# When batches are made ready, who adds the weight blocks, and when TensorE loads its step registers, in a one-core decoder layer

## The reference

```python
x = x + attn(layernorm(x), ...)                  # linear attention, 16 heads
x = x + experts(layernorm(x), itok, ctx, ctx, ctx)   # one of 4 experts per token
x = x + ffn(layernorm(x), W_up, W_gate, W_down)
# experts: e = token id // (25000 // 4)
g = silu(h @ ctx[e].T); u = h @ ctx[e].T; y = (g * u) @ ctx[e].T
# ffn: each weight is clip(round(W / s), -1, 1) * s with s = mean(|W|)
hidden = silu(x @ wu.T) * (x @ wg.T)             # 512 -> 2048
return hidden @ wd.T
```

## Time and profile before

| | |
|---|---|
| time, median of 3 runs | 760.04 us (760.04 to 761.48) |
| profiled execution, its own time / span | 760.04 / 758.1 us |
| PE, PEld, DVE, ACT, POOL busy | 695.5, 457.6, 503.4, 295.2, 250.6 us |
| idle of PE before the region products of line 1482 | 28.5 us in 3 waits |
| experts' stage, first product to first up product | 264.3 to 404.6 us |
| feed-forward stage | 404.6 to 758.1 us |

### The profile page before, as it was taken

One profiled execution on the slowest core, in us unless ns is written; L12 is line 12 of the kernel. 1 busy time (PEld: TensorE's weight loads), 2 busy tenths in 40 slices (PEclk: granted clock), 3 DMA queues, 4 the chain that ended last, 5 costly groups with the idle time before them and its releaser, 6 DMA issues.

```text
span 758.1 us, 12681 instructions
## 1 busy us (share of the span) xinstructions
PE 695.5 (92%) x4745; PEld 457.6 (60%) x4776; DVE 503.4 (66%) x814; ACT 295.2 (39%) x450; POOL 250.6 (33%) x242
## 2 busy tenths in 40 slices
PE   7999999999998799999889999499977999499995
PEld 5565456556564656665447777377755777377772
DVE  5566766766757565567756978388773978457664
ACT  4365554554545244443322433234332343123330
POOL 4204523333334600003640343435431543414222
PEclk9999999999999999999999999899997999899998
DMA  8924035036046587601220030202111120201001
GB/s 246 338 81 142 1 128 206 0 125 208 1 155 234 166 326 253 243 29 42 50 50 1 1 51 1 49 1 81 25 26 25 52 54 1 50 1 56 1 1 55
DMA packets 57910, 67.37 MB, mean 89 GB/s; under 512 B 35072, under 2 KB 35072, under 8 KB 56832
## 3 DMA queue, kind: packets, MB, share of 16 engines
q1 hardware_dynamic: 54016, 54.03, 23.5%
q0 software_dynamic: 3840, 12.59, 4.4%
HBM read 46.69 MB, written 12.59 MB: 78 GB/s over the span
## 4 chain that ended last, share of the span: by engine, by line
PE 74%; DVE 9%; issue 7%; ACT 4%; DMA 2%; SPq 1%; POOL 1%; another core or an unknown queue 0%; POOLq 0%; DVEq 0%; ACTq 0%
PE bank L1211 26%; PE bank L1482 25%; PE bank L1491 13%; PE bank L1204 4%; PE bank L1404 2%; DVE region L829 2%; PE bank L1368 2%; PE bank L1382 2%; DMA w_att<-stage 2%; DVE late L825 1%; DMA stage<-in_L_attn_Wv_dram 1%; ACT stage L639 1%; ACT stage L519 1%; DVE region L833 1%; ACT tmp L527 1%
## 5 line engine op out<-in xcount | busy, mean ns | idle before, releaser
L1482 PE MATMUL bank<-w_att,region 128*128 128x256 f16 x1024 | 130.9, 277 | 28.5 <-issue 28.5
L1482 PEld LDWEIGHTS bank<-w_att,region 128*128 128x128 bf16 x1024 | 101.6, 99 | 48.7 <-issue 29.9
L1491 PE MATMUL bank<-region,w_moe 128*128 128x512 bf16 x481 | 115.5, 383 | 3.9 <-DVE w_moe L1122 2.1
L1132 DVE TENSOR_TENSOR n<-bank,n 128x512 f32<-128x512 f32 x112 | 71.7, 685 | 55.8 <-PE bank L1482 54.2
L1211 PE MATMUL bank<-late,w_att 128*128 128x512 f16 x384 | 86.8, 382 | 2.0 <-DVE region L872 1.9
L445 POOL TENSOR_TENSOR w_moe<-tmp,w_moe 128x512 f16<-128x512 f32 x30 | 36.0, 1200 | 154.3 <-ACT w_moe L669 154.3
L1491 PEld LDWEIGHTS bank<-region,w_moe 128*128 128x128 f16 x512 | 50.5, 99 | 51.2 <-DVE w_moe L1122 2.6
L326 POOL TENSOR_SCALAR ve<-mv 128x1 f32<-128x1 f32 (+2 forms) x29 | 10.9, 377 | 198.4 <-DVE mv L709 198.3
L662 ACT ACTIVATE n<-n,qs 128x512 f32<-128x512 f32 x64 | 44.5, 718 | 71.8 <-DVE n L1132 71.3
L1482 PE MATMUL bank<-w_att,late 128*128 128x256 f16 x512 | 68.6, 279 | 0.0
L1211 PEld LDWEIGHTS bank<-late,w_att 128*128 128x128 f16 x384 | 37.4, 98 | 45.0 <-DVE region L872 2.7
(11 more groups left out here) (161 smaller groups left out, 1143.1 us busy)
## 6 DMA issues: line engine op xcount, KB each, us to landing
stage<-in_L_ffn_W_up_dram SPq DMA_DIRECT2D x8, 1024.0 KB
stage<-in_L_ffn_W_gate_dram SPq DMA_DIRECT2D x8, 1024.0 KB, 5.4
rows<-sorted_residual SPq DMA_DIRECT2D x4, 1026.0 KB, 8.6
stage<-in_ctx_dram SPq DMA_DIRECT2D x4, 1024.0 KB, 6.6
stage<-in_L_ffn_W_down_dram SPq DMA_DIRECT2D x4, 1024.0 KB
nrm<-in_L_ffn_W_down_dram SPq DMA_DIRECT2D x4, 1024.0 KB, 8.0
n<-sorted_tokens SPq DMA_DIRECT2D x16, 256.0 KB, 5.8
rows<-in_x_dram SPq DMA_DIRECT2D x1, 3072.0 KB, 18.6
```

Source lines behind the costliest of these rows:

```text
L1132: dve.tensor_tensor(out, wk_ps[(14 * n + m) % 4][:, :], other, ALU.add).then_inc(s["up_add"], 1)
L1482: mm = pe.matmul(wk_ps[bank][:, q * H:(q + 1) * H], w[:, c + q, k * P:(k + 1) * P], x3S_part[slot][:, h, m, k], start=(h == 0 and k == 0), ...
L1491: mm = pe.matmul(ffy_ps[t][:, :], hid[:, u, h, q, (t % 2) * P:(t % 2 + 1) * P], tern[2][:, c + q], start=(begins and q == 0 and h == 0), s ...
```

## The change

Four things are edited.

1. Batch preparation moves one group ahead: a half is normalised, summed and sent in t = 0 or t = 2 instead of t = 1 or 3, and its stats and rsqrt are one group before that (for half 2 in step 15; for halves 4 and 6 in t = 3 of the batch before).
2. Gate's four weight sums move from GpSimd to VectorE, each beside up's. Of the eight, S1 are in steps 10 and 11, both S3 in 13, both S2 in 16, both S4 in 17, always behind `h_lo`.
3. In the last group (n = 15), `downs_before(2)` is done behind gate 6 instead of ahead of gate 4.
4. TensorE loads the registers of step i + 1 (expert and offset) behind the xs transposes of step i, ahead of `second(i - 1)`, keeps the expert's register, and `second` uses it without a load of its own.

```diff
+        third_rsqrt(2)
...
             if b + 1 < B and t % 2 == 0:
-                third_rsqrt(2 * b + 2 + t // 2)
-            if b + 1 < B and t % 2 == 1:
                 x3_lo(2 * b + 2 + t // 2)
+            if (b + 1 < B and t == 1) or (b + 2 < B and t == 3):
+                third_rsqrt(2 * b + 3 + t // 2)
...
-            if b + 1 < B and t % 2 == 1:
+            if b + 1 < B and t % 2 == 0:
                 x3_hi(2 * b + 2 + t // 2)
...
+            nxt = 2 * b + 2 + t // 2 if b + 1 < B and t % 2 == 0 else None
+            then = 2 * b + 3 + t // 2 if t == 1 and b + 1 < B or t == 3 and b + 2 < B else None
...
         def expert_step(i, experts, off):
             first(i, experts[i], off)
             if i + 1 < NT:
                 xs_transpose(i + 1)
+            if i + 1 < STEPS:
+                experts.append(expert_of(i + 1))
+                off = offset_of(i + 1)
             if i > 0:
                 second(i - 1, experts[i - 1])
...
-            downs_before(2)
+            if n < NT - 1:
+                downs_before(2)
             gate(4, S1, 3)
             gate(5, A22, 6)
             gate(6, S4, 2)
+            if n == NT - 1:
+                downs_before(2)
             downs_before(3)
```

More of the change, by code:

```diff
@@ L429, in x3_lo @@
             pool.tensor_tensor(x3h[:, 1], x3_flat[:, 0:7 * H], x3h[:, 0], ALU.subtract).then_inc(s["x3_lo"], 1)
[L431 to L434, removed]
         def send_out(b):
@@ L1064, in x3_sums, with weight_sum @@
             less(6, 1, 5)
-        def up_sum(dst, a, b, op, n):
+        def weight_sum(j, n):
+            done = "gate_sums" if j else "up_sums"
+            dst, a, b, op = ((S1, A21, A22, ALU.add), (S3, A11, A21, ALU.subtract), (S2, S1, A11, ALU.subtract),
+                             (S4, A12, S2, ALU.subtract))[n]
             if n > 0:
-                dve.wait_ge(s["up_sums"], n)
-            dve.tensor_tensor(dst, a, b, op).then_inc(s["up_sums"], 1)
+                dve.wait_ge(s[done], n)
+            dve.tensor_tensor(dst[j], a[j], b[j], op).then_inc(s[done], 1)
         def expert_step(i):
@@ L1093, in expert_step @@
                 dve.wait_ge(s["unit_copy"], 12 * T)
-                up_sum(S1[0], A21[0], A22[0], ALU.add, 0)
-            if i == 12:
-                up_sum(S3[0], A11[0], A21[0], ALU.subtract, 1)
+                weight_sum(0, 0)
+            if i == 11:
+                weight_sum(1, 0)
+            if i == 13:
+                weight_sum(0, 1)
+                weight_sum(1, 1)
             if i == 15:
-                up_sum(S2[0], S1[0], A11[0], ALU.subtract, 2)
+                x3_stats(2)
             if i == 16:
-                up_sum(S4[0], A12[0], S2[0], ALU.subtract, 3)
+                weight_sum(0, 2)
+                weight_sum(1, 2)
+            if i == 17:
+                weight_sum(0, 3)
+                weight_sum(1, 3)
         xs_lo(0)
@@ L1127, in group @@
             ends = n == NT - 1
-            nxt = 2 * b + 2 + t // 2 if b + 1 < B else None
+            nxt = 2 * b + 2 + t // 2 if b + 1 < B and t % 2 == 0 else None
+            then = 2 * b + 3 + t // 2 if t == 1 and b + 1 < B or t == 3 and b + 2 < B else None
             def up_of(out, m, other):
@@ L1148, in group @@
                 finish(b - 1, (2, 3), (16 * b, 16 * b))
-            if nxt is not None and t % 2 == 1:
+            if nxt is not None:
                 x3_normalise(nxt)
@@ L1157, in group @@
             up_of(u12, 6, u12)
-            if nxt is not None and t % 2 == 0:
-                x3_stats(nxt)
-            if nxt is not None and t % 2 == 1:
+            if then is not None:
+                x3_stats(then)
+            if nxt is not None:
                 x3_sums(nxt)
@@ L1438, in xs_transpose, with expert_of, offset_of, weights_of @@
             transposes(tx_ps, lambda k: xs_slot[i % 3][:, k * P:(k + 1) * P]).then_inc(s["tx_mm"], 1)
-        def weights_of(i):
-            e = pe.value_load(step_expert[0:1, i:i + 1], min_val=0, max_val=E - 1)
+        def expert_of(i):
+            return pe.value_load(step_expert[0:1, i:i + 1], min_val=0, max_val=E - 1)
+        def offset_of(i):
+            return pe.value_load(step_off[0:1, i:i + 1], min_val=0, max_val=(B - 1) * 2 * K * S + S - P)
+        def weights_of(e):
             return lambda i, j, k: w_moe[:, bass.ds(e, 1), j, k].rearrange("p a d -> p (a d)")
-        def first(i):
-            w = weights_of(i)
-            off = pe.value_load(step_off[0:1, i:i + 1], min_val=0, max_val=(B - 1) * 2 * K * S + S - P)
+        def first(i, e, off):
+            w = weights_of(e)
             pe.wait_ge(s["xs_lo"], min(i, NT - 1) + 1)
@@ L1450, in first, with second @@
             product(z_ps[:, :], lambda i, j, k: sorted_T[:, bass.ds(off + (i * K + k) * S, P)], w).then_inc(s["z_mm"], 1)
-        def second(i):
-            w = weights_of(i)
+        def second(i, e):
+            w = weights_of(e)
             pe.wait_ge(s["h_lo"], i + 1)
@@ L1456, in second, with expert_step @@
             product(y_ps[:, :], lambda i, j, k: hT[:, i, k * P:(k + 1) * P], w).then_inc(s["y_mm"], 1)
-        def expert_step(i):
-            first(i)
+        def expert_step(i, experts, off):
+            first(i, experts[i], off)
             if i + 1 < NT:
                 xs_transpose(i + 1)
+            if i + 1 < STEPS:
+                experts.append(expert_of(i + 1))
+                off = offset_of(i + 1)
             if i > 0:
-                second(i - 1)
+                second(i - 1, experts[i - 1])
             if i == 0:
@@ L1470, in expert_step @@
             transposes(th_ps, lambda k: h32[:, k * P:(k + 1) * P]).then_inc(s["th_mm"], 1)
+            return off
         pe.wait_ge(s["route_ready"], 3)
+        experts, off = [expert_of(0)], offset_of(0)
         xs_transpose(0)
         for i in range(STEPS):
-            expert_step(i)
+            off = expert_step(i, experts, off)
         def part(bank, w, c, slot, m):
@@ L1535, in group @@
             if n == 0:
-                second(STEPS - 1)
+                second(STEPS - 1, experts[STEPS - 1])
             up(2, A12, 1)
```

5 lines of the change are left out of this document (removed).

## The result

The changed kernel takes **716.65 us** (median of 4 runs, 716.13 to 718.61), where before takes 760.06 us beside it (4 runs). The ratio is 0.943, 95% interval 0.941 to 0.945: faster by 5.7%. The profiled execution has a span of 714.3 us, 43.8 us less than before. The forecast was 718.9 us.

What follows compares the result with a forecast made beforehand. The prediction took TensorE, busy nine tenths of the span, as the bound, leaving its waits to gain. Its terms, -34.5 + 2.2 - 3.7 - 2.4 - 2.7 = -41.1 us, took 760.04 to 718.9 us, range 714 to 725.

Steps and rivals of the forecast that it cites:

- Batches one group earlier: Feed-forward stage, three batch ends: the late transfer into `w_att` moves one group ahead and all three waits go, -34.5 us.
- The first group: Second `downs` of group 1: TensorE stands for the third `hid_lo`, delayed by `x3_lo` and a later VectorE, +2.2 us.
- The registers, steps 1 to 10: Experts' stage: with two register loads no longer between th and `first`, `first` starts without its delay, -3.7 us.
- the Trainium skill's sentence: Register loads: other engine instructions can be queued during a control instruction, so moving the loads would give 0 instead of 3.7.
- Steps 10 to 18: Experts' stage, weight sums on VectorE: 6.3 us at most can be had, 4.0 stay through slow loads and VectorE, -2.4 us.
- In steps 13 and 16 such transfers run still, and there TensorE's sequencer has no lead: Experts' stage: loads beside transposing transfers hold up `second` by 1.7 and 1.3 us.
- The end: Last group: earlier gates let VectorE start 1.3 us sooner, and the clock holds for 1.5 us, -2.7 us.
- The clock's part: Last matmuls: idle shrinks from 2.10 to about 1.2 us, so the clock holds and slow weight loads go, 1.5 us.
- Everything in the experts' stage is covered: Rival: transfers end before the loads, steps 10 to 18 take 52.8 us, no stop in group 0; 712.8 us, chance 0.10.
- The loads only change place: Rival, experts' stage: the sequencer has no lead, so `second` stands for what `first` no longer does; 725.0 us, chance 0.08.
- S3's form: Rival, step 13: S3 is slow by its form, not through GpSimd, 7.1 us more; 726.0 us, chance 0.04.

Runs made afterwards that it cites:

- the kernel that takes the cause away: Changed kernel, but in group 0 GpSimd writes all four `hid_lo` before `x3_lo`; 715.17 us.
- the kernel with four: Changed kernel with every step's pair of register loads done twice, four loads in the new place; 725.15 us.
- Two kernels with the old 2.10 us: Kernel before with batch preparation one group earlier alone, 729.39 us; changed kernel with the last group's third `downs` ahead of gate 4 again, 718.45 us.
- the second of these kernels: Changed kernel with sorted tile 3 sent ahead of SyncE's scatter wait and, in group 0, all four `hid_lo` ahead of `x3_lo`; 714.65 us.

## Why the prediction was right

The total is 2.2 us below the forecast, inside the range. That it came so near is in part luck: steps 10 to 18 gave 3.8 us more than forecast, the ten steps before them 1.2 less and the start 0.5 less, and these partly offset each other. By its steps:

- **Batches one group earlier, -34.5.** Right to 0.1 us (-34.45), the slow stretches behind the stops included.
- **The first group, +2.2.** Right in mechanism, place and releaser; the size is 1.71 (1.57 by the kernel that takes the cause away). `x3_lo` took 4.05 us as said, but the third `hid_lo` started 23.2 us behind the first up product and not 23.5.
- **The registers, steps 1 to 10, -3.7.** Right in mechanism, too large: -2.5 over these ten (81.12 to 78.64). Steps 4 to 10 give 2.48 us, about as much as they had to give, with `first` 0.44 us behind th. The first three gave nothing together, because in step 2 the lead that I took for granted was gone where the sequencer had waited for a transfer. The arithmetic that I held against the Trainium skill's sentence proved nothing, since it works on the registers just loaded; the stops ahead of `second` do. And I had no term for the start: the two loads for step 0 now stood ahead of the first transposes, not behind them. They delay these by 1.1 to 1.4 us. Of this, 0.5 us is left at `first`(0), since in the profile before ScalarE had a unit's copy to do first, which started at 262.32, over a microsecond after these transposes.
- **Steps 10 to 18, -2.4.** The term that was mis-sized: -6.15, at my bound of -6.3. The nine steps took 53.00 us, and I had 52.8 for no wait at all. Both S3 took 1.2 us, as taken. With gate's sums back on GpSimd 3.1 us return, with the loads back 4.4, so the two overlap. The step that failed is "In steps 13 and 16 such transfers run still, and there TensorE's sequencer has no lead". I took every load during a transfer as a slow one, from the single 1041 ns. In the changed kernel they fell 0.1 to 0.8 us behind an issue or 3.1 us and more, where they cost 0.30 us, and at that length they fit behind `first` and the transposes even without a lead. That this hangs on the moment and not on the new place as such shows in the kernel with four: there, in the same place, two fall into the slow stretch of step 13. The pairs of sums held nothing up either.
- **The end, -2.7.** The sum is right (-2.9), the split was not. 1.3 us are the order, as taken. The clock's part, 1.6 us, I put down to the shorter idle stretch. Two kernels with the old 2.10 us keep the clock, so that reason was wrong. The part came with edit 1, in all traces that have it; why is not shown.
- **The rivals.** "Everything in the experts' stage is covered" (712.8) was right for steps 10 to 18 and wrong for group 1. "The loads only change place" falls, as does S3's form. From the first up product to the last matmul the clock stayed full.

## What to carry to other kernels

A register load holds TensorE's sequencer for about 0.7 us. It costs nothing where enough work is queued ahead of it (here 2.4 us of loads behind twelve matmuls and four transposes), and up to all of it behind anything that the sequencer itself has waited for, above all a transfer that arrives just in time: put the loads ahead of such a wait. When work is moved ahead a group, look for the first group, which is shorter than the rest; taking one instruction out of its way there gave back 1.57 of 1.71 us. And before a wait is charged to a transfer, compare the moments, not only the lengths: here a load beside the same transfer took 0.30 or 0.98 us, 0.7 us apart.

## What the runs showed of the hardware

- In steps 10 to 18 a register load on TensorE was slow (0.58 to 1.05 us instead of 0.30) from 1.2 to 2.6 us behind the issue of a transposing transfer that lands after 4.3 us, and nowhere else. It is not the only case: at the start of the experts' stage, with no such transfer, the pair took 1.29 and 0.43 us. No run here shows the cause of either.
- The same idle stretch of 2.10 us before the same matmuls came with weight loads at the lower level once and at the full clock twice. Likewise 1.53 us of idle came ahead of `first`(0): in eight kernels the product behind it took 2.8 us five times and 4.13 to 5.30 us three times.
- A 256 KB tile took 11.49 and 14.54 us on the chain, from its issue on, where transfers of 1 MB were issued around it; the median of such transfers in the second of these kernels was 5.7 us.
- VectorE's normalising took 1.18 us alone and 3.95 us beside a 4.07 us sum on GpSimd.
